# Moving the four corner products of an attention step from its head to the middle of the score pass

## What is computed

```
q, k = rope(x @ Wq), rope(x @ Wk)              # 32 and 8 heads of dimension 8
scores = einsum('bkgtd,bksd->bkgts', qg, k) / sqrt(8)
scores = where(causal, scores, -inf)
attn = softmax(scores, axis=-1)
ctx = einsum('bkgts,bksd->bkgtd', attn, v)
x = x + layernorm(ctx @ Wo + b_out)
x = x + layernorm(ffn(layernorm(x)))           # shared and routed experts
```

## Time and profile before

| | us |
|---|---|
| median of 3 runs | 666.75 |
| the three runs | 665.57, 670.29, 666.75 |
| span of the profiled execution, first to last instruction | 665.1 |
| attention steps 0 to 63, by the start of their second pass | 45.3 to 244.6 |
| PE busy in the span | 633.5 (95%) |
| DVE busy in the span | 531.7 (80%) |
| ACT busy in the span | 417.6 (63%) |
| POOL busy in the span | 324.8 (49%) |

### The profile page before, as it was taken

The page is one execution under the profiler, slowest core; times in us unless marked ns, Lnnn a source line. Parts: engine busy times, 40 slices in busy tenths (PEclk is TensorE's granted clock), DMA queues, the critical chain, the costliest instruction groups (busy, mean ns, idle before and its releaser), DMA issues.

```text
span 665.1 us, 15276 instructions
## 1 busy us (share of the span) xinstructions
PE 633.5 (95%) x5914; PEld 514.7 (77%) x5914; DVE 531.7 (80%) x1052; ACT 417.6 (63%) x782; POOL 324.8 (49%) x519
## 2 busy tenths in 40 slices
PE   8987899999999979999989999999999999999994
PEld 6753455555655547888889999999999999888883
DVE  5689999999988743479868888888988888468895
ACT  2426788888887875542257777787877787422230
POOL 3225657767666762100375454545454530178854
PEclk9989999999999999999999999999999999999998
DMA  3853633645550000000376786777776773032221
GB/s 100 165 126 69 113 83 67 129 99 155 103 89 18 19 10 17 17 0 1 119 246 224 239 288 217 260 247 249 249 263 237 248 235 138 24 90 85 88 65 47
DMA packets 79672, 87.10 MB, mean 131 GB/s; under 512 B 54353, under 2 KB 69073, under 8 KB 79601
## 3 DMA queue, kind: packets, MB, share of 16 engines
q0 software_dynamic: 11872, 54.53, 24.9%
q1 hardware_dynamic: 67456, 31.21, 19.5%
q10 hardware_dynamic: 272, 0.39, 0.2%
HBM read 63.83 MB, written 9.31 MB: 110 GB/s over the span
## 4 chain that ended last, share of the span: by engine, by line
PE 75%; DVE 11%; issue 3%; ACT 3%; SPq 2%; DMA 2%; POOL 2%; DVEq 0%; POOLq 0%; another core or an unknown queue 0%; ACTq 0%
PE PS L542 71%; DVE NM L1034 3%; DVE NM L1030 2%; PE PS L553 2%; PE PS L748 1%; DMA X<-in_x 1%; ACT PF L889 1%; SPq L1543 1%; POOL PF L1452 1%; POOL RS L1395 1%; SPq L1549 1%; DMA XG<-xn,XIDX 1%; DVE X L1299 1%; PE PS L697 1%; DVE RR L995 1%
## 5 line engine op out<-in xcount | busy, mean ns | idle before, releaser
L1239 DVE TENSOR_TENSOR HF<-SS,PS 128x256 f32<-128x256 f32 (+2 forms) x141 | 68.6, 487 | 68.4 <-ACT SS L935 29.1
L1318 DVE TENSOR_TENSOR WL<-RAW,WH 128x768 fp32r<-128x768 f32 x125 | 118.4, 958 | 4.4 <-ACT WH L844 3.7
L935 ACT ACTIVATE SS<-PS 128x256 f32<-128x256 f32 (+2 forms) x141 | 62.0, 439 | 81.3 <-PE PS L542 69.6
L1452 POOL TENSOR_SCALAR_AFFINE_SELECT PF<-PF 128x512 f32<-128x512 f32 x128 | 83.5, 677 | 56.0 <-ACT PF L889 55.4
L542 PE MATMUL PS<-WH,HH 128*128 128x256 f32 x355 | 103.2, 291 | 1.2 <-DVE HL L1332 1.0
L844 ACT ACTIVATE HH<-HF 128x256 fp32r<-128x256 f32 (+1 forms) x120 | 58.0, 484 | 72.5 <-DVE HF L1239 61.6
L844 ACT ACTIVATE WH<-RAW 128x768 fp32r<-128x768 f32 x125 | 103.3, 841 | 0.0
L889 ACT ACTIVATE PF<-PS 128x1536 f32<-128x1536 f32 x64 | 92.9, 1452 | 16.5 <-PE PS L542 14.8
L542 PE MATMUL PS<-WL,HH 128*128 128x256 f32 x355 | 100.3, 282 | 0.0
L542 PE MATMUL PS<-WH,HL 128*128 128x256 f32 x355 | 100.2, 282 | 0.0
L542 PE MATMUL PS<-XGL,WH 128*128 128x256 f32 x320 | 90.5, 283 | 0.0
(11 more groups left out here) (203 smaller groups left out, 1468.4 us busy)
## 6 DMA issues: line engine op xcount, KB each, us to landing
ys<-YO SPq DMA_DIRECT2D x16, 256.0 KB
RAW<-in_wsh SPq DMA_DIRECT2D x4, 768.0 KB, 5.0
XT<-in_xt SPq DMA_DIRECT2D x8, 256.0 KB, 3.6
X<-in_x SPq DMA_DIRECT2D x8, 256.0 KB, 3.8
xn<-YY SPq DMA_DIRECT2D x16, 128.0 KB, 1.7
out<-X SPq DMA_DIRECT2D x16, 128.0 KB
ys<-YO SPq DMA_DIRECT2D x7, 128.0 KB
RAW<-in_wsh SPq DMA_DIRECT2D x2, 384.0 KB, 4.8
```

The costliest lines, as they stand in the source:

```text
L935: eng.activation(ss, both(i, bank(b))[0], ACT.Silu).then_inc(free[b] if dense(i) else silu, 1)
L1239: eng.tensor_tensor(hf, ss, both(c, bank(b))[1], ALU.mult).then_inc(free[b], 1)
L1318: eng.tensor_tensor(WL[q % 2][:, c], RAW[raw_of(q)][:, c], WH[q % 2][:, c].bitcast(F32), ALU.subtract).then_inc(w_lo, 1)
L1452: eng.affine_select(out=o, in_=o, pattern=[[0, 4], [1, 128]], base=0, channel_multiplier=-1, compare_op=ALU.is_ge, fill=0.0).then_inc(zero ...
```

## The change

The corner products for k = n + 7 and the waits that stand with them (the turned queries and keys have landed, the bank is free) move from the stage `early(k)` at the head of step n into `pass2(n)`: behind its first two products, and ahead of `tops` of side 0. For the first seven k nothing changes. The number of instructions is the same on every engine, and so are the banks.

```diff
-            def early(k):
-
+            def shaped(k):
                 turned_in(e, 2 * (k // 8))
                 c = take(("early", k))
                 corners(bank(c).rearrange("p (a t) -> p a t", a=4))
+                return c
+
+            def early(k):
+
                 if k < LEAD:
+                    c = shaped(k)
                     tops(k, c, 0).then_inc(top0, 1)
...
                 k = n + LEAD
-                c = use["early", k][0] if k < 64 else None
                 mm(v[:, 0, :, :], side(n, 0, 128, 256), heads(n, 0, 128, 256), True).then_inc(right0, 1)
                 mm(o[1], side(n, 1, 0, 128), heads(n, 1, 0, 256), True)
                 if k < 64:
+                    c = shaped(k)
                     tops(k, c, 0).then_inc(top0, 1)
```

## The result

The changed kernel takes 673.75 us (median of 5 runs, 673.47 to 674.43) against 666.75 (median of 5 runs too, 665.57 to 670.29); the ratio is 1.0092 with a 95% interval of 1.0065 to 1.0118. It is slower: the medians are 7.0 us apart, and the ratio makes it 6.1 us (4.3 to 7.9). The profiled execution has a span of 672.7 us, 7.6 above the one of before; it was itself the slowest of the five (674.43).

The account below looks back on a forecast made before the run. TensorE was taken to bound the attention from about step 13 on, VectorE before it. 57 steps x 0.19 = 10.8 us, less 3.9 absorbed, left 6.9 on 666.75: 673.7 us, range 668.5 to 677.

Parts of the forecast that it names:

- (b): Corners inside the second pass: start at 0.32, `tops` of side 0 at 0.47 to 0.48; +0.19 to +0.20 us per step.
- (c): Behind the corners: side 1's `tops` still wait for `top0`, so the rest of the step moves equally; +0.19 taken.
- (d): Waits ahead of the early corners: letting two products pass there gives nothing back.
- (e): Exponential before the next second pass: margin shrinks from 0.37 to 0.20 us in a short step, still enough; zero cost.
- Rival 4: Exponential's 0.20 margin is too small, some 20 short steps wait 0.1 each: 675.7 us; chance 0.07.
- my list: Extra TensorE time absorbed by waits for other engines, step by step through the attention; 3.9 us in all.
- Rivals 1 to 3: Corners overlap side 1, 664.9 us, chance 0.08; VectorE hides half, 670.3, 0.17; nothing absorbed, 677.6, 0.08.

Follow-up runs that it names:

- the two partial moves: The change made only from step 13 on, and only in steps 0 to 12, each against the kernel before: ratios 1.0088 and 1.0008.
- `tops` ahead of the 512 columns: Against the kernel with corners behind the second pass's first product: side 0's `tops` moved ahead of side 1's 512-column product; 669.48 us, 1.0036 to the kernel before.
- the added products: Kernel before plus zero-adding products ahead of side 0's `tops`: four 32x32 products, ratio 1.0252, or one 64x128 product, ratio 1.0016.
- the waits at the head: Against the changed kernel: corners stay inside the second pass, their waits return to the head of the step; 672.22 us, 1.0101 to the kernel before.
- the two versions with fewer changes of shape: Against the kernel before: late corners also at the head from k = 7 on, ratio 1.0233; all twelve corners in one block behind the second pass, 1.0151.
- the corners behind the first product: Against the changed kernel: corners behind only the second pass's first product, ahead of side 1's 512 columns; 673.27 us, 1.0119 to the kernel before.
- `tops` at the head: Kernel before with side 0's `tops` at the head of the second pass and side 1's ahead of its right block: 671.11 us, ratio 1.0005.

## Why the prediction was right

- **The size.** Forecast 673.7, measured 673.75. In ratios 1.0104 was forecast and 1.0092 measured.
- **The bound.** TensorE from step 13 on, VectorE ahead of it: the two partial moves show 1.0088 and 1.0008. Of the 7.6 us between the two profiled spans, 7.1 arose between steps 13 and 57.
- **(b), the corners in the middle.** Predicted 0.32 and 0.47 to 0.48, measured 0.32 and 0.48. Both terms were shown apart: one gap more alone costs 0.09 (`tops` ahead of the 512 columns), and a change of shape does not start until the other half of the rows is done (the added products). Per step 0.20, where I took 0.19.
- **(c), the rest of the step** moved with `top0`, 0.35 behind. The signal for the right block of side 1 won nothing, as said.
- **(d), the waits.** The run with the waits at the head agrees with zero.
- **(e), the exponential** never became the bound: of PE's idle time in front of the second pass over the attention, 2.3 us in all (2.4 before), 0.7 was released by the exponential (0.5 before). In a short step of the changed kernel the exponential ends at 208.01 and the next pass starts at 208.20: 0.19, where the prediction had 0.20. Rival 4 is out.
- **What others' waits took.** From step 13 on 44 steps x 0.20 = 8.8 us arrived as 7.1: 1.7 absorbed, where my list gave 2.0. Step by step, by the starts of the second pass: steps 16 and 17 took up 0.5 (listed 0.5), the six steps 23 to 43 took up 0.9 (listed 0.9), steps 44 and 45 together 0.24 (listed 0.4; PE's wait for VectorE fell from 0.89 to 0.60 us only), and step 56, listed with 0.2, took up nothing. In the first 13 steps I left 0.6 us, and 0.4 was measured, too little for its interval to exclude zero. By the profile, then, the price of a step (0.20 for 0.19, some 0.4 us over 44 steps) and what is absorbed (1.7 for 2.0) were both off in the direction of a longer time, together by some 0.7 us. That the predicted 673.7 meets the median of 673.75 so closely is partly luck: it is nearer than these terms are known, and the spans of the two profiled executions differ by 7.6 where the medians differ by 7.0.
- **Rivals 1 to 3** each fail on a number: corners at 0.32 and not under 0.2; 0.64 more in four steps and not half of it; 7 us and not 10.8.

The chance split was between within and over 1%, at 0.47 and 0.51, and the interval of the ratio has the bound of 1% inside it.

## What to carry to other kernels

Group matrix products by the shape of their array tile, and price each change of shape at its gap plus whatever the other row groups are still doing: a few small products of another shape, dropped between two long ones that share the array, cost far more than their columns. Read the starts of products, not their busy time, for this. But before regrouping, ask which banks the group now needs earlier and who frees them: here the two versions with fewer changes of shape lost more by waits than the gaps are worth. And look at what stands ahead, in the program, of a product whose end another one waits for: it can delay the signal.

## What the runs showed of the hardware that I had not expected

- **A product can start ahead of earlier ones on other rows.** In the changed kernel the right block of side 1 starts at 158.63, although the second `tops` of side 0 (158.69) and the left block of side 0 (158.75) stand ahead of it in the program. The Trainium skill, TensorE: Matmul & The Clock Gate, Part 3, says that matmuls are in strict order in start and end; the trace disagrees for the start, and the run with `tops` ahead of the 512 columns agrees for the end.
- **A signal waits for the program's order.** Exchanging two products that start together moved the waiting product from 0.84 to 0.72.
- **TensorE's clock in the early steps.** The window of 53 to 63 us of the kernel before (columns as in the earlier trace rows):

```profile
53.00:63.00 10.00, 6.92 (x105) 3.59 (x102) 9.75 (x20) 6.76 (x9) 4.76 (x8) 1.00 0.09 17
```

The same window of the changed kernel:

```profile
53.00:63.00 10.00, 9.55 (x85) 3.97 (x84) 9.76 (x20) 5.79 (x8) 3.91 (x8) 0.51 0.02 4
```

After the change TensorE ran at the lower of its two levels (0.51 on average, 1.2 GHz for nearly all of it) where it had run at 2.4 GHz. Both kernels had run at the lower level once before, near the start of the attention (0.66 on average from 45 to 50 us in both); in the changed kernel PE was then busy 2.26 us of the three from 50 to 53, and from 52.7 to 62.8 us the granted clock was 0.50. VectorE, which is the bound there, was busy 9.75 and 9.76 us of ten with 20 instructions in both, so in this window VectorE lost hardly anything by it. What such a stretch costs in the end is not shown. The profiled execution with the move in steps 0 to 12 has one too (0.50 from 54.5 to 64 us); it took 667.68 us, 2.2 above the median of its twelve, and of these twelve the two with the lowest granted clock over the whole execution (0.984 and 0.981) were the slowest (667.68 and 668.63). So it may cost some 2 us in an execution that has it; the profiles also differ by as much in these steps at other clocks.

In the same window the granted clock was 0.66 with the waits at the head, 0.71 with the corners behind the first product, 0.72 with `tops` at the head, 0.83 with the added 64x128 product, 0.93 with `tops` ahead of the 512 columns, 1.00 with the added 32x32 products and 1.00 with the move from step 13 on. The kernel with `tops` at the head has its corners where the kernel before has them, so the move is not needed for such a stretch. What sets the stretches off I can't say. They stand ahead of step 13, and the comparisons of steps 13 to 57 are free of them.
